# A macaron transformer block on one core: 144 identity products ahead of TensorE's waits, and one written order for the whole program

## The reference

```python
x = x + 0.5 * _L0_ffn_ref(_layernorm(x, axis=-1), ...)   # low rank 32, gelu
x = x + _L0_attn_ref(_layernorm(x, axis=-1), ...)        # 16 heads of 8, causal softmax, layer norm, Wo
x = x + 0.5 * _L0_ffn_ref(_layernorm(x, axis=-1), ...)
x = x + 0.5 * _L1_ffn_ref(_layernorm(x, axis=-1), ...)   # shared expert + 2 of 8 routed experts
x = x + _L1_attn_ref(_layernorm(x, axis=-1), ...)        # Taylor linear attention, 16 heads
x = x + 0.5 * _L1_ffn_ref(_layernorm(x, axis=-1), ...)
```

## Time and profile before

| | |
|---|---|
| median of three runs | 1490.75 us (1488.5 to 1492.01) |
| the profiled execution | 1486.09 us, of which the span of its instructions is 1484.4 us |
| PE busy in the span | 1242.9 us (84%) |
| DVE, ACT, POOL busy | 950.1, 725.7, 417.7 us |
| mean granted clock of PE | 0.934 |

### The profile page before, as it was taken

How to read it: one execution, slowest core, us unless ns; L and a number is a source line. 1 busy time by engine, 2 the same in 40 slices (tenths; PEclk the granted TensorE clock), 3 DMA queues, 4 the chain that set the end, 5 groups by cost and what they waited for, 6 DMA issues and landing times. The chain is left out here.

```text
span 1484.4 us, 26633 instructions
## 1 busy us (share of the span) xinstructions
PE 1242.9 (84%) x10064; PEld 705.9 (48%) x10064; DVE 950.1 (64%) x2923; ACT 725.7 (49%) x1247; POOL 417.7 (28%) x707
## 2 busy tenths in 40 slices
PE   5698668987789887899878887798878998879998
PEld 3354234444544455444554445544455445543456
DVE  6985377446974469834797347964488646874267
ACT  3165335643366433664346543465435663456533
POOL 1023101640026400264003540035300362016730
PEclk9699779998999989999999999899998999999999
DMA  3100001000010000100001000010010100011000
GB/s 117 43 2 2 8 22 34 11 8 7 23 44 2 8 13 17 44 1 9 19 11 44 1 9 22 8 44 2 8 29 1 44 2 1 13 38 44 2 2 15
DMA packets 37201, 28.75 MB, mean 19 GB/s; under 512 B 7960, under 2 KB 36304, under 8 KB 37072
## 3 DMA queue, kind: packets, MB, share of 16 engines
q1 hardware_dynamic: 37072, 27.04, 6.7%
HBM read 5.90 MB, written 2.10 MB: 5 GB/s over the span
## 5 line engine op out<-in xcount | busy, mean ns | idle before, releaser
L775 ACT ACTIVATE left<-bank 128x512 f32<-128x512 f32 x280 | 159.9, 598 | 86.3 <-PE bank L1237 84.5
L968 DVE TENSOR_REDUCE left<-bank 128x4 f32<-128x512 f32 x280 | 184.5, 682 | 22.6 <-PE bank L1218 21.8
L819 ACT ACTIVATE right<-bank 128x512 f32<-128x512 f32 x280 | 158.6, 598 | 82.2 <-PE bank L1324 80.1
L689 POOL TENSOR_SCALAR_AFFINE_SELECT left<-left 128x512 f32<-128x512 f32 (+1 forms) x144 | 82.5, 587 | 397.6 <-ACT left L775 382.7
L1160 PE MATMUL bank<-right,pairs 128*128 128x512 f16 x588 | 161.6, 399 | 17.3 <-DVE right L1047 10.1
L1216 PE MATMUL bank<-left 128*128 128x512 f16 (+1 forms) x448 | 123.3, 324 | 42.4 <-DVE left L968 25.9
L709 POOL TENSOR_SCALAR right<-right 128x1024 f32<-128x1024 f32 x168 | 151.9, 904 | 14.7
L689 POOL TENSOR_SCALAR_AFFINE_SELECT right<-right 128x256 f32<-128x256 f32 (+1 forms) x240 | 99.3, 426 | 133.3 <-ACT right L819 122.8
L1350 PE MATMUL bank<-right 128*32 128x256 f32 (+3 forms) x1792 | 134.6, 439 | 0.0
L1068 DVE SCALAR_TENSOR_TENSOR right<-bank,right 128x128 f32<-128x128 f32 x448 | 125.8, 343 | 11.7 <-PE bank L1300 6.4
L1300 PEld LDWEIGHTS bank<-ew,right 128*128 128x128 f32 x896 | 113.8, 191 | 25.8 <-DVE right L1057 12.5
(11 more groups left out here) (274 smaller groups left out, 2201.8 us busy)
## 6 DMA issues: line engine op xcount, KB each, us to landing
right<-right SPq DMA_DIRECT2D x168, 64.0 KB, 2.0
left<-left SPq DMA_DIRECT2D x168, 32.0 KB, 1.8
left<-x_dram SPq DMA_DIRECT2D x7, 256.0 KB, 2.6
out_dram<-right SPq DMA_DIRECT2D x7, 256.0 KB, 2.2
left<-left SPq DMA_DIRECT2D x24, 64.0 KB, 2.0
right<-right SPq DMA_DIRECT2D x24, 32.0 KB, 1.9
wo<-wo_dram SPq DMA_DIRECT2D x1, 512.0 KB, 3.7
ew<-ew_dram SPq DMA_DIRECT2D x1, 512.0 KB, 4.6
```

Of the source, the lines that this page charges most:

```text
L689: return pool.affine_select(out=v, in_=v, compare_op=ALU.is_ge, fill=fill, base=0, pattern=[[0, heads], [1, P]], channel_multiplier=-1)
L775: act.activation(h.probs[:, g % 2, u * S:(u + 1) * S], ps[:, :], ACT.Exp).then_inc(h.act, 1)
L819: act.activation(h.wts[:, p % 2, u * S:(u + 1) * S], ps[:, :], ACT.Square, bias=1.0, scale=FEAT ** -0.5).then_inc(h.act, 1)
L968: dve.tensor_reduce(h.bmax[:, u * NT:(u + 1) * NT], ps[:, :].rearrange("p (b k) -> p b k", k=P), AX.X, ALU.max).then_inc(h.dve, 1)
```

## The change

The three strings of each engine become one for the whole program (SECTIONS, LOOP), so that the five repetitions of the body no longer share an order. The lists of steps within a stream stay as they were; only how the two sides are woven changes. On PE 443 of 1632 steps stand at another place than before, 325 of them by one place and none by more than seven; on DVE 213 of 936, on ACT 299 of 1096, on POOL 122 of 344, on SP 10 of 64.

A table, WARM, names 26 steps on PE. In front of each, after the wait for its bank and before the wait for its operand, PE multiplies the 128 x 128 f32 identity with itself 2 to 16 times, 144 times in all, into the bank that the step then overwrites. For this the wait for the bank is moved ahead of the wait for the operand. At `up0` and an odd number (`up0 1`) the operand's wait has been passed already, so that there the products stand only behind the wait for the bank.

```diff
-SECTIONS = {
-    "begin": {"L": listing(("A1", 0, ORDER_A), ("A1", 1, FRONT)), "R": listing(("A2", 0, ORDER_A))},
-    "body": {"L": listing(("A1", 1, BACK), ("A1", 2, FRONT)), "R": listing(("B2", 0, ORDER_B))},
-    "finish": {"L": listing(("A1", B - 2, BACK), ("B1", 0, ORDER_B)),
-               "R": listing(("B2", B - 3, ORDER_B), ("B2", B - 2, ORDER_B))},
+TURNS = B - 3
+
+
+def turns_of(body):
+
+    return [(name, turn + i, step) for i in range(TURNS) for name, turn, step in body]
+
+
+SECTIONS = {"all": {
+    "L": (listing(("A1", 0, ORDER_A), ("A1", 1, FRONT)) + turns_of(listing(("A1", 1, BACK), ("A1", 2, FRONT)))
+          + listing(("A1", B - 2, BACK), ("B1", 0, ORDER_B))),
+    "R": (listing(("A2", 0, ORDER_A)) + turns_of(listing(("B2", 0, ORDER_B)))
+          + listing(("B2", B - 3, ORDER_B), ("B2", B - 2, ORDER_B))),
+}}
+
+WARM = {
+    ("A1", 0, "up0 1"): 6, ("A2", 0, "down0 0"): 8, ("A1", 0, "low 1"): 6, ("A2", 0, "out0"): 4,
+    ("A1", 0, "down0 2"): 4, ("A1", 1, "norm 0"): 12, ("A1", 1, "low 0"): 4, ("A2", 0, "down0 3"): 4,
+    ("A1", 1, "max 0"): 12, ("B2", 0, "split 2"): 2, ("B2", 0, "router 1"): 6, ("A1", 2, "exp 0"): 2,
+    ("B2", 1, "split 2"): 2, ("B2", 1, "router 1"): 4, ("B2", 2, "split 0"): 4, ("A1", 3, "up0 1"): 2,
+    ("A1", 3, "shift 0"): 2, ("B2", 2, "router 1"): 6, ("B2", 3, "split 0"): 8, ("A1", 4, "up0 1"): 2,
+    ("B2", 3, "scale 4"): 4, ("B2", 3, "router 1"): 6, ("B2", 4, "router 1"): 4, ("B2", 5, "split 0"): 8,
+    ("A1", 6, "down0 0"): 6, ("B2", 6, "split 0"): 16,
 }
-TURNS = B - 3
 
 LOOP = {
-    "begin": {
+    "all": {
         "pe": """
             LLLLRRRRLRLLRLRLRRLLLLRRRRLLLLLLLLLLLLLLLLLLRRRRRRRRRRRRLRLRRLRRRLLRRLRRLRLRRLLLRRRLLRRRLLLLRLLLRRLL
-            RLRLRLRLLLRLLRRRLLLRRRLLRRLRLRRLRLRLLRLLLLRRLLRRLLLRRLLLLRRLLRLRRLRRRLLLRLRRRLRLRRLLRRLLLLLRLLLLRLRL
-            RRRLRRRRRRRRLLLRRRLRRRLLLLRRRLRLLLRRRRLLLLRLLLRLLRRLLLLLLLLLL
+            RLRLRLRLLLRLLRRRLLLRRRLLRRLRLRRLRLRLLRLLLLRRLLRRLLLRRLLLLRRLLRLRRLRRRLLLRLRRRLRLRRLLRRLLLLRLLLLRRLLL
+            RRRLRRRRRRRLLLRRRLRRRRLLLLRRRLRLLLRRRRLLLLLRLLRLLRRLLLLLLLLLLLLLLLRRRRLLRRLLLLRLLLRRLRRLRRRRLLRLLLLL
...
 
-            steps(fns, 0, "begin", engine)
-            for i in range(TURNS):
-                steps(fns, i, "body", engine)
-            steps(fns, 0, "finish", engine)
...
+            def warm(h, it, step, ps):
+
+                for _ in range(WARM.get((h.name, it, step), 0)):
+                    mm(ps[:, 0:P], ident[:, :], ident[:, :], start=True, stop=True)
+
             def norm(h, it, k, step):
 
+                ps = fill(passed, h, it, step, "lnT")
+                warm(h, it, step, ps)
                 passed.wait_ge(h.ln_ready, it * h.lns + k + 1)
-                ps = fill(passed, h, it, step, "lnT")
                 for t in range(NT):
                     last = nc.tensor.transpose(ps[:, t * P:(t + 1) * P], h.ln[:, t, :], ident[:, :])
                 last.then_inc(h.filled, 1)
@@ -1162,16 +1198,19 @@
...
             def low(h, it, n, step):
 
+                ps = fill(passed, h, it, step, "p")
+                warm(h, it, step, ps)
                 passed.wait_ge(h.act, drained(h, it, f"norm {(0, 3)[n]}", "lnT"))
-                ps = fill(passed, h, it, step, "p")
                 mm(ps[:, :], u1[:, :], h.lnT[:, :], start=True, stop=True).then_inc(h.filled, 1)
 
             def up0(h, it, n, step):
                 passed.wait_ge(v1_split, 1)
-                passed.wait_ge(h.dve, drained(h, it, f"low {n // 2}", "p"))
                 for unit, _ in ring_uses(step):
                     f = int(unit[2:])
                     ps = fill(passed, h, it, step, unit)
+                    if f % 2 == 0:
+                        warm(h, it, step, ps)
+                        passed.wait_ge(h.dve, drained(h, it, f"low {n // 2}", "p"))
                     mm(ps[:, :], v1s[:, f * P:(f + 1) * P], h.low[0:3 * R0, :], start=True, stop=True)\
                         .then_inc(h.filled, 1)
 
...
                     ps = fill(passed, h, it, step, "mix")
+                    warm(h, it, step, ps)
                     passed.wait_ge(h.act, drained(h, it, f"up0 {n + 1}", "up3"))
...
             def router(h, it, n, step):
                 passed.wait_ge(w_split, 1)
+                ps = fill(passed, h, it, step, "router")
+                warm(h, it, step, ps)
                 passed.wait_ge(h.dve, drained(h, it, f"split {(0, 2)[n]}", "lnT"))
-                ps = fill(passed, h, it, step, "router")
                 for t in range(NT):
...
             def scale(h, it, p, step):
 
+                ps = fill(passed, h, it, step, "r")
+                warm(h, it, step, ps)
                 passed.wait_ge(h.rrows_ready, it * 2 + p // GP + 1)
-                ps = fill(passed, h, it, step, "r")
                 mm(ps[:, :], spread[:, p % GP, :], h.rrows[:, :], start=True, stop=True).then_inc(h.filled, 1)
```

More of the change, by code:

```diff
@@ L173 @@
             LLLLLLLLLLLLRRRRRRRRRRRRRRRRRRRRRRLLLLLLLLLLLLLLLLLLLLLLLRRRRRRRRRRRRRRRRRRRRRRRLLLLLLLLLLLLLLLLLLLL
[L174 to L203, removed]
@@ L553, in run @@
         def run(eng, fns, engine):
-            steps(fns, 0, "begin", engine)
-            for i in range(TURNS):
-                steps(fns, i, "body", engine)
-            steps(fns, 0, "finish", engine)
+            steps(fns, 0, "all", engine)
         def fill(pe, h, it, step, unit):
@@ L1196, in qkv0 @@
                 passed.wait_ge(tables, 2 * GH + 2)
-                passed.wait_ge(h.act, drained(h, it, "norm 1", "lnT"))
                 for name, wt in (("q", wq0), ("k", wk0)):
                     ps = fill(passed, h, it, step, name)
+                    if name == "q":
+                        warm(h, it, step, ps)
+                        passed.wait_ge(h.act, drained(h, it, "norm 1", "lnT"))
                     mm(ps[:, :], wt[:, :], h.lnT[:, :], start=True, stop=True).then_inc(h.filled, 1)
@@ L1209, in rowmax @@
                 g, u = divmod(n, NU0)
+                ps = fill(passed, h, it, step, "s")
                 if u == 0:
+                    warm(h, it, step, ps)
                     passed.wait_ge(h.kpad0_ready, it * NG + g + 1)
-                ps = fill(passed, h, it, step, "s")
                 for kt, j in UNITS0[u]:
@@ L1222, in shift @@
             def shift(h, it, g, step):
+                ps = fill(passed, h, it, step, "mT")
+                warm(h, it, step, ps)
                 passed.wait_ge(h.rmax_ready, it * NG + g + 1)
-                ps = fill(passed, h, it, step, "mT")
                 for t in range(NT):
@@ L1259, in out0 @@
             def out0(h, it, n, step):
+                ps = fill(passed, h, it, step, "y")
+                warm(h, it, step, ps)
                 passed.wait_ge(h.act, drained(h, it, "norm 2", "lnT"))
-                ps = fill(passed, h, it, step, "y")
                 for t in range(NT):
```

124 lines of the change are left out of this document (85 added, 39 removed).

## The result

The changed kernel took 1472.99 us (median of 4 runs, 1467.71 to 1476.39) against 1489.62 for the kernel before on the same chip (1483.41 to 1492.01): a ratio of 0.9894 (95% interval 0.9866 to 0.9922). That is 1.06% less; the forecast, 1476.7 against 1490.75, was 0.94% less.

What follows compares the result with a forecast made beforehand. No engine is full throughout: PE, DVE or low-clock chains of short steps limit different stages. Terms -2.0 - 3.0 - 3.5 - 7.0 + 1.5 = -14.0 us gave 1472.1 us, 1476.7 at the median; range 1460 to 1493.

Steps and rivals of the forecast that it cites:

- (c): Where B2 begins, DVE's new order fills its 5.08 us wait for A1's `qkv0` transfers: -3.5 us.
- (f): The rest of the order: swaps of neighbouring steps of the two sides, 0 us, bounds -6 and +6.
- (a): At the start, products keep the clock up for `norm 1` and the wq and wk products: -2.0 us.
- (b): From the first A sequences to the next, products speed A1's chain: -3.0 us, bounds -5.4 and +2.8.
- (d): Body and end: products lift the clock in six of twelve slow stretches, -9 less a cost of 2: -7.0 us.
- (e): Last B2 sequence: sixteen products ahead of a 0.20 us wait delay `split 0`: +1.5 us, bounds 0 and +3.8.
- only long waits: Rival: only long waits lower the clock, so short sites are useless; 1487 us at the median, chance 0.05.
- The clock falls later instead: Rival: the clock falls at the next wait, so no change, 1488 to 1493 us; chance 0.12.
- The first rival: The clock holds nearly everywhere in the chains: -25.5 us, 1465 us at the median; chance 0.25.

Runs made afterwards that it cites:

- e3_nine: The changed kernel with identity products only at the first nine sites (60 of 144); 1479.69 us, 0.9944 of the kernel before.
- e4_no16: The changed kernel without the sixteen products ahead of the last B2 sequence's `split 0`; 1469.93 us, 0.9863 of the kernel before.
- e2_products: The kernel before, in its old order, with all 144 identity products added; 1472.15 us, 0.9881 of the kernel before.
- e15_old_more: The kernel before, in its old order throughout, with 234 identity products added; 1459.89 us, 0.9813 of the kernel before.
- run 6: Two kernels with more products in remaining waits: `e12_more`, 1456.84 us, and `e15_old_more`, 1459.89 us.
- e14_start: New order at start and end only, 128 products less the 14 at the first two sites; 1469.26 us, 0.9878 of the kernel before.
- e12_more: New order at start and end only, 128 products plus 114 more in remaining waits; 1456.84 us, 0.9795 of the kernel before.
- run 3: New order by pieces, 128 products each: none 1474.08 us, start 1470.0, start and end 1465.08, body alone 1481.18.

## Why the prediction came out, step by step

The sum holds by groups. Order, then nine sites, then sixteen more are three runs of one set; the last step compares with the changed kernel's own set.

| steps | forecast, us | by the medians, us |
|---|---|---|
| (c) and (f), the order alone | -3.5 | -4.3 |
| (a) and (b), the first nine sites | -5.0 | -3.4 |
| (d), sixteen sites | -7.0 | -9.8 |
| (e), the last site | +1.5 | +3.1 |
| sum | -14.0 | -14.4 |

The result's own set gave -16.6, and its interval reaches from -11.6 to -20.0. That the sum came out so near is in part luck, since terms that were off cancelled.

- **(a), mis-sized.** The clock rose where it was meant to, and "A2's result is not needed by DVE until after A1's layer norm, so that costs nothing" held: in `e3_nine` A2's `down0 0` is pushed back as well (28.39 for 26.95), and its `centre 1` is not late. What failed is "the DVE stretch behind them starts that much earlier": the 2.0 us were 1.0 to 1.6, because DVE had A2's layer norm ahead of A1's copies and waited for PE only 0.68 us there. That `pad0` was 0.41 us late in the changed kernel's trace comes from A2's `low 0`, which ran at the lower level ahead of the first product.
- **(b), right** in size: 4.2 us for 3.0 in the trace, though `low 0` and `down0` stayed at the lower level; other traces with the same products spread from 0.8 to 4.8. Its upper bound is not what its terms add up to: 1.0 + 0.15 + 1.5 is 2.65, and 5.3 at twice the cost, not 2.8.
- **(c), right:** 3.59 us for 3.5, and the order alone has it too.
- **(d), right** in mechanism and mis-sized: the term "I let six stretches go: -9" less a cost of 2. The runs gave 9.8. Its count was off as well. The trace of before has five such passages, not six, and the products with wq and wk could not give 1.8 us there, a number from the start; wk took 1.21 us behind this wq, and both take 1.02 at full clock:

```profile
722.69 1.91 PE L1200 MATMUL bank<-left,wq 128*128 128x512 f32 x2
```

  So ten stretches could give some 12 us, not 18, but seven of them went and not six: in the changed kernel both `down0` and the transposes are at full clock in three of the five passages, the products with wq and wk in four.
- **(e), not shown.** It took a wait of 0.20 us from the order of before; in the new order it is 2.50, and up to `router 0` the traces show no cost. The 3.1 us of the medians lie between the bounds of 0 and 3.8, but are not clear of the noise. In the old order the delay of 3 us is real and is made up.
- **(f), right by cancelling.** "A swap hands one step's length from one stream to the other" holds for the sum and not for the parts: the body's order cost 7.1 us, and by the medians the end's gave 4.9. The bound of one us for a repetition was too small for the body.

Of the rivals, "only long waits" fell with the sixteen later sites: 36 of their 68 products stand in waits of 1.4 to 1.6 us, as in the earlier trace rows, and sixteen in two of 3.48 and 3.84 us; ahead of the first of these two the trace of `e4_no16` has already gone from 3.46 us behind `e3_nine` (at 393 us) to 5.74 ahead (at 707). "The clock falls later instead" fell with them. The first rival, the clock held nearly everywhere, is not this kernel, but its direction is right: with 114 more products and a better order the time is 1456.84 us.

The Trainium skill (TensorE: Matmul & The Clock Gate, Terms) prices the lower clock by its total time, at half of it here. Three kernels with the order of before test that, each by the means of clock and span over all its runs: the kernel before (first set) 0.929 and 1486.2 us, so 212 us at the lower level; `e2_products` 0.9545 and 1470.3 us, 134; `e15_old_more` 0.9618 and 1458.3 us, 111. The first 78 us less brought 15.9, where the page's price, an estimate, is 39; the next 23 us brought 12.0, where it is about 12. So the runs disagree with it in the first step and agree in the second: a microsecond at the lower level has no single price here. That it depends on which steps lie in it is what the rows of single places suggest, and run 6.

## What to carry to other kernels

Price a lower clock by the steps that lie on the path in it, not by its mean, and put filler where PE waits for data, with a bank already in hand. Read the length of that wait in the order that will run, not in the old one (0.20 and 2.50 us). Before blaming a delay on a change, go back to the first row that is late: at the start it stood ahead of every product. Test a new order piece by piece, since a gain at the ends can hide a loss in the middle.

## What was not expected of the hardware

- The place of the lower clock is not fixed by the work near it: A1's first `down0` took 1.06 us in the kernel before (at 23.93 us) and 1.93 in `e14_start`, both without products ahead of it, while `norm 1` went the other way (1.12 and 0.66). A2's first `low 0` took 1.02 us in `e3_nine` and 1.92 in the changed kernel, with the same steps ahead of it.
- The mean clock does not order kernels: 0.957 at 1471.0 us of span (`e2_products`) and at 1457.3 (`e12_more`). Their orders differ too; by the medians of run 3 the new order at both ends is worth 9.0 of these 13.7 us.
